# Selective-scan kernel on one core: another order of the sixteen states, three spread inflows, two decay tiles, six rows of C through a ring

## The chip, the cores and the metric

One core of a Trainium2 chip (trn2) runs the whole program. The metric is the device time of one execution in microseconds (us); lower is better.

## The reference, cut to what matters

A layer norm with modulation gives x_ssm (B=4 batches, 1024 tokens, 512 features). From it two selective state-space models are computed, one over the tokens forwards and one backwards, each with E=1024 channels and N=16 states a channel, and gated and projected back. The part that costs the time:

```
def _ssm(u, Wdbc, Wdt, bdt, Alog, Dp):
    dbc = einsum('bse,re->bsr', u, Wdbc);  dlt, Bm, Cm = split(dbc, [R, R + N])
    delta = softplus(einsum('bsr,er->bse', dlt, Wdt) + bdt)
    dA  = exp(delta[..., None] * -exp(Alog))                  # decay, N a channel
    dBu = delta[..., None] * Bm[:, :, None, :] * u[..., None] # inflow, N a channel
    h[t] = dA[t] * h[t-1] + dBu[t]                            # scan over t
    y[t] = sum over n of h[t, n] * C[t, n]                    # product and sum
    return y + u * Dp
out = x + gate * ((silu(mx) * (z1 + flip(z2))) @ Wf.T + bf + x_ssm)
```

## The kernel before, in words

All data is fp32, and everything around the scan is folded into it. A setup part (lines 28 to 485) folds weights, normalises tokens and writes the rows of B and C of each direction to DRAM. The main part (`ssm_kernel`) goes through 64 **units**. A unit k is one batch, one direction and 128 of the 1024 channels, with the 1024 tokens along the free axis: of each 16 units of a batch, the first 8 are forward in time and the next 8 backward. A unit has 16 **steps** c = 0 to 15, one for each state; q = 16k + c counts them through. Each engine has its own program, written out by hand as a loop over k and c with `if c == ...` for all side work; the engines meet only through semaphores, and each executes its own list strictly in order.

For a state four things are made: a decay (ScalarE, an exp of delta, line 1195), an inflow, a scan (VectorE, line 1326), and a product with the row of C, after which TensorE transposes it and adds it into the PSUM tile `y` (`sum_chunk`, line 885, four steps later, LAG). The string `KINDS` (line 487) says for each step how that is shared out:

- **E** (spread): TensorE makes the inflow by multiplying the transposed du with a diagonal matrix of B (`spread_inflow`, line 903; 8 products in fp32, which the trace shows as 16 instructions) into a PSUM slot. ScalarE makes the diagonals once a direction and batch (`make_diagonal`, line 1144, 8 instructions each).
- **A** (scaled): ScalarE scales the transposed du by B in two halves of four instructions (`scale_half`, line 1127, at the steps that `SCALE_STEPS` gives), and TensorE transposes the result into the slot (`turn_inflow`, line 893, 8 instructions).
- **V** and **P**: GpSimd multiplies the row of B, loaded by DMA into the ring `bst`, with du (line 1234). The decay goes into the PSUM slot.

For E and A the decay goes into the one tile `dec`, and GpSimd makes the product in place in `hbuf` (line 1239), as it does for P. For V VectorE scans into the slot and makes the product itself (line 1335). There are two slots; step q uses slot q % 2, so whatever writes it waits until step q - 2 has left it (`wait_scanned_out`, line 619): for a V that is the end of VectorE's product, for the others the end of the scan. `hbuf` is a ring of five. The 16 rows of C are resident in `cres` for a direction and batch, and are reloaded at its end (`load_c`, line 694, in SyncE's list); rows of B are loaded in a ring of four (`load_b`, line 688).

Side work in the same lists: the next unit's delta (TensorE at step 3; ScalarE's `softplus_start` and `softplus_end` at steps 4 and 5, right behind ScalarE's copy of the last y at step 4; VectorE's line 1260 at step 5, between the scan and the product of that step), and its z product (`z_part`), which feeds du (VectorE line 1270 and TensorE's `turn_du`, line 925). There are two kinds of unit:

- in **forward units** (k % 16 = 1 to 8) z is at steps 7 to 10, and an x product (`mx_part`, line 864) at steps 13, 14, 15 and the next 0. ScalarE makes its sigmoid in two halves, behind the decays of step 15 and of the next step 1 (`sigmoid_half`, line 1106), VectorE a silu from it.
- in **backward units** (k % 16 = 9 to 15 and 0) z is at steps 9 to 12; TensorE turns y back at step 7 for VectorE's gating at step 7 (line 1292), and makes the output projection of a token block (line 969) at steps 15 and the next 0, for which gated tiles are loaded in SyncE's list at step 13 (line 712), and of which VectorE reads the result at the next step 1. In the first batch work on B and C (`make_dbc`) stands in its place.

TensorE's list at a step is: the inflow of this state (A or E), skip terms at step 4, the sum of the state four steps back, then the side work.

Of the kernel before, what the change touches and what calls it, by code (L numbers as in the profile page):

```python
# [12 lines left out]
P = 128  # L13
# [3 lines left out]
ET = E // P  # L17
# [7 lines left out]
NU = 2 * B * ET  # L25


def setup_kernel(nc, t, scratch):

    with ExitStack() as ctx:  # L30
# [358 lines left out]
        def _(pe):  # L389
# [93 lines left out]
            for c in range(2):  # L483
# [3 lines left out]
KINDS = "EVAVEVAPAVAPAPAV"  # L487
SCALE_STEPS = {0: ((2, 0), (2, 1)), 3: ((6, 0),), 5: ((6, 1),), 6: ((8, 0),), 7: ((8, 1),), 8: ((10, 0),),
               9: ((10, 1),), 10: ((12, 0),), 11: ((12, 1),), 12: ((14, 0),), 13: ((14, 1),)}
SPREAD = [n for n in range(N) if KINDS[n] == "E"]  # L490
SEQ = ET * N
HR = 5
LAG = 4
DR = 2
# [25 lines left out]

INFLOWS_AT = {q: [i for i in range(DR, len(POOLED)) if inflow_step(i) == q] for q in range(NU * N)}


def ssm_kernel(nc, t, scratch):

    with ExitStack() as ctx:
# [3 lines left out]
        def sem(name):  # L530
# [3 lines left out]
        cres = sb("cres", [P, N, S])  # L534
# [3 lines left out]
        soft, ud, yrd, silu, ybuf, dec, dut = (sb(n, [P, S]) for n in (  # L538
            "soft", "ud", "yrd", "silu", "ybuf", "dec", "dut"))
# [14 lines left out]
        c_in = [sem(f"c_in{n}") for n in range(N)]  # L554
        last_in = sem("last_in")
# [60 lines left out]
        def z_bank(k, h):  # L616
            return mb[h] if k > 0 else y[:, half(h)]

# [52 lines left out]
        def _(sp):  # L671
# [22 lines left out]
            def load_c(g, n):  # L694
                sp.dma_start(cres[:, n, :],
                             scratch["bc"][g % 2, g // 2, N + n, :].partition_broadcast(P)).then_inc(c_in[n], 16)

# [39 lines left out]
            for n in range(3):  # L737
                load_c(0, n)

            for k in range(NU):  # L740
# [3 lines left out]
                for c in range(N):  # L744
# [4 lines left out]
                    if k == 0 and c + 3 < N:  # L749
                        load_c(0, c + 3)  # L750
                    if k == ET and c == 0:
                        sp.dma_start(wproj.rearrange("p a k r -> p (a k r)"), scratch["wproj"]).then_inc(pj_in, 16)
                        sp.dma_start(dbias, scratch["dbias"]).then_inc(pj_in, 16)
# [35 lines left out]
                    if k == NU - 1 and c >= ET:  # L789
                        wait_product(sp, q - ET)  # L790
                        sp.dma_start(skip_tile(TAIL + c - ET), scratch["xs"][NC - 2 + (c - ET) // TB, :, c % TB, :]).then_inc(rest_in, 16)
                        sp.dma_start(x_tile(TAIL + c - ET), t["xT"][TAIL + c - ET]).then_inc(rest_in, 16)
# [27 lines left out]
                    if e == ET - 1 and k + 1 < NU and c >= 5:  # L820
                        wait_product(sp, q - 5)
                        load_c(k // ET + 1, c - 5)
                    if e == 0 and k >= ET and c < 5:
                        wait_product(sp, q - 5)
                        load_c(k // ET, N - 5 + c)
# [255 lines left out]
        def _(act):  # L1081
# [94 lines left out]
            make_diagonal(0, 1)  # L1176

            for k in range(NU):
                f, zs = wtile(k), z_step(k)
                new_b = (k + 1) % ET == 0  # L1180
                for c in range(N):
# [3 lines left out]
                    if kind(q) in "AE":  # L1185
                        if before("AE", q) > 0:
                            act.wait_ge(scanned, TURNED[before("AE", q) - 1] + 1)
                        decays = dec[:]
# [10 lines left out]
                    if c == 1 and k > 0 and k % ET == 0:  # L1199
                        make_diagonal(k // ET, 1)  # L1200
# [27 lines left out]
        def _(pool):  # L1228
# [7 lines left out]
            def product(q):  # L1236
                pool.wait_ge(c_in[q % N], 16 * (q // SEQ + 1))
                pool.wait_ge(scanned, q + 1)
                nc.gpsimd.tensor_tensor(hbuf[:, q % HR, :], hbuf[:, q % HR, :], cres[:, q % N, :],  # L1239
                                        ALU.mult).then_inc(pool_prod, 1)  # L1240
# [14 lines left out]
        def _(dve):  # L1255
# [55 lines left out]
            for k in range(NU):  # L1311
                zs = z_step(k)
                step = -1 if backward(k) else 1
                for c in range(N):
                    q = N * k + c
                    dve.wait_ge(decay_ready, q + 1)
                    if kind(q) in "AE":
                        dve.wait_ge(turned, before("AE", q + 1))
                        decays, inflows = dec, slot[q % 2]
# [12 lines left out]
                    if kind(q) == "V":  # L1332
                        dve.wait_ge(scanned, q + 1)
                        dve.wait_ge(c_in[c], 16 * (q // SEQ + 1))
                        nc.vector.tensor_tensor(hbuf[:, q % HR, :], slot[q % 2][:], cres[:, c, :],  # L1335
# [91 lines left out]
```

## Time and profile before

| | |
|---|---|
| median of 3 runs | 3288.13 us (3287.22 to 3289.47) |
| profiled execution | 3287.01 us, its span 3285.2 us |
| busy: VectorE | 3017.2 us, 92% |
| busy: TensorE, matmuls | 2993.0 us, 91% |
| busy: GpSimd | 2903.7 us, 88% |
| busy: ScalarE | 2678.5 us, 82% |
| granted TensorE clock, mean | 0.985 of 2.4 GHz |
| moved by DMA | 560.40 MB |

The setup takes the first 255 us or so, up to the first scan, and what follows the last scan some 58 us. Between them lie the 64 units (unit 20, a forward one, and unit 28, a backward one, are looked at below; unit 8 is the first after a change of direction), so that 1 us more or less in every unit is 64 us. The profiled execution can be set against the median directly: they are 1.1 us apart.

### The profile page before, as it was taken

The page shows a single profiled execution, that of the slowest core. Times are in us where ns is not written, and L with a number is a line of the kernel's source. Part 1 is how long each engine was busy: PE and PEld are TensorE (multiplying, and loading weights), DVE is VectorE, ACT ScalarE, POOL GpSimd, SP SyncE. Part 2 cuts the span into 40 slices and gives each one's busy share as a digit, 9 for nine tenths or more (in the row PEclk, how much of TensorE's full clock was granted, in tenths as well). Part 3 has the DMA queues.
Part 4 walks back from the last instruction along what each step waited for, and adds up shares of the span by engine and source line. Part 5 has one row for each costly group of instructions (what it writes and reads, how often), then busy time and mean ns, then how long its engine had stood idle before and what let it go on. Part 6 is the DMA issues. An engine that isn't in the chain of part 4 may idle for free.

```text
span 3285.2 us, 54883 instructions
## 1 busy us (share of the span) xinstructions
PE 2993.0 (91%) x19924; PEld 2375.2 (72%) x19924; DVE 3017.2 (92%) x2008; ACT 2678.5 (82%) x5151; POOL 2903.7 (88%) x1288
## 2 busy tenths in 40 slices
PE   8887999899998999899999999899998999899999
PEld 5765666677677666678877767678777666677789
DVE  2838999999999999999999999999998999999994
ACT  1448999988888999987788999987877999988772
POOL 1528999999999999999999999999998999999993
PEclk9989999999999999999999999999999999999999
DMA  5775334644476333645465334645566343645463
GB/s 224 236 244 171 136 117 137 227 154 163 162 248 207 130 123 131 228 144 163 159 243 192 130 123 134 224 139 165 165 217 207 120 132 130 232 136 163 156 198 111
DMA packets 207053, 560.40 MB, mean 171 GB/s; under 512 B 20200, under 2 KB 66472, under 8 KB 202560
## 3 DMA queue, kind: packets, MB, share of 16 engines
q1 hardware_dynamic: 203424, 538.01, 48.5%
q0 software_dynamic: 2304, 16.78, 1.3%
q8 instruction: 159, 2.61, 0.3%
q10 hardware_dynamic: 1056, 2.10, 0.2%
q14 instruction: 110, 0.90, 0.1%
HBM read 476.19 MB, written 80.63 MB: 169 GB/s over the span
## 4 chain that ended last, share of the span: by engine, by line
PE 49%; ACT 20%; DVE 12%; issue 10%; POOL 1%; DVEq 0%; ACTq 0%; POOLq 0%
PE y L888 14%; PE slot L899 10%; PE mb L859 9%; ACT abuf L1134 8%; PE mb L969 6%; DVE hbuf L1326 6%; ACT slot L1195 3%; DVE hbuf L1335 3%; PE mb L869 3%; PE slot L911 3%; DVE slot L1326 3%; ACT dec L1195 2%; PE mb L930 1%; ACT soft L1090 1%; ACT yrd L1125 1%
## 5 line engine op out<-in xcount | busy, mean ns | idle before, releaser
L1239 POOL TENSOR_TENSOR hbuf<-hbuf,cres 128x1024 f32<-128x1024 f32 x704 | 1664.4, 2377 | 143.9 <-DVE hbuf L1326 143.8
L1234 POOL TENSOR_TENSOR bst<-bst,du 128x1024 f32<-128x1024 f32 x512 | 1220.2, 2383 | 46.7 <-DVE du L1270 46.7
L1326 DVE TENSOR_TENSOR_SCAN hbuf<-dec,slot 128x1024 f32<-128x1024 f32 x512 | 1165.0, 2275 | 40.3 <-PE slot L911 27.2
L888 PE MATMUL y<-ident,hbuf 128*128 128x128 f32 x8192 | 1016.0, 273 | 1.8 <-POOL hbuf L1239 1.7
L888 PEld LDWEIGHTS y<-ident,hbuf 128*128 128x128 f32 x8192 | 923.9, 141 | 106.4 <-issue 103.5
L1134 ACT ACTIVATE abuf<-dut,bt 128x128 f32<-128x128 f32 x3072 | 964.7, 387 | 0.0
L1326 DVE TENSOR_TENSOR_SCAN slot<-slot,bst 128x1024 f32<-128x1024 f32 x320 | 728.3, 2276 | 22.5 <-ACT slot L1195 22.1
L1195 ACT ACTIVATE slot<-delta,par 128x1024 f32<-128x1024 f32 x512 | 568.4, 1110 | 199.6 <-DVE hbuf L1335 186.6
L1195 ACT ACTIVATE dec<-delta,par 128x1024 f32<-128x1024 f32 x512 | 584.2, 1141 | 118.7 <-DVE hbuf L1326 118.1
L899 PE MATMUL slot<-ident,abuf 128*128 128x128 f32 x3072 | 408.6, 276 | 170.8 <-ACT abuf L1134 160.1
L899 PEld LDWEIGHTS slot<-ident,abuf 128*128 128x128 f32 x3072 | 339.0, 141 | 303.4 <-ACT abuf L1134 243.0
L859 PE MATMUL mb<-xn,wzs 128*128 128x512 f32 x1008 | 478.9, 597 | 15.2 <-DVE ybuf L1292 11.7
L1326 DVE TENSOR_TENSOR_SCAN hbuf<-slot,bst 128x1024 f32<-128x1024 f32 x192 | 434.7, 2264 | 0.1
L1335 DVE TENSOR_TENSOR hbuf<-slot,cres 128x1024 f32<-128x1024 f32 x320 | 390.7, 1221 | 8.0
L911 PEld LDWEIGHTS slot<-diag,dut 128*128 128x128 f32 x2048 | 260.2, 203 | 106.3 <-issue 102.9
L911 PE MATMUL slot<-diag,dut 128*128 128x128 f32 x2048 | 269.6, 288 | 43.0 <-DVE hbuf L1326 40.1
L859 PEld LDWEIGHTS mb<-xn,wzs 128*128 128x128 f32 x1008 | 171.6, 190 | 146.3 <-issue 144.2
L869 PE MATMUL mb<-xn,wx 128*128 128x512 f32 x512 | 240.9, 593 | 0.0
L969 PE MATMUL mb<-ybuf,wf 128*128 128x128 f32 x1504 | 179.0, 278 | 5.0 <-issue 4.1
L969 PEld LDWEIGHTS mb<-ybuf,wf 128*128 128x128 f32 x1504 | 174.6, 194 | 5.4 <-issue 4.3
L848 PE MATMUL mb<-dl,wdt 81*128 81x512 f32 x256 | 135.1, 632 | 17.2 <-DVE silu L1280 10.0
L869 PEld LDWEIGHTS mb<-xn,wx 128*128 128x128 f32 x512 | 87.3, 190 | 61.2 <-issue 61.2
(157 smaller groups left out, 2301.3 us busy)
## 6 DMA issues: line engine op xcount, KB each, us to landing
bst<-bc_s SPq DMA_DIRECT2D x512, 512.0 KB, 3.9
cres<-bc_s SPq DMA_DIRECT2D x128, 512.0 KB, 6.8
wzs<-wz_s SPq DMA_DIRECT2D x64, 256.0 KB, 4.0
yf_s<-yrd SPq DMA_DIRECT2D x32, 512.0 KB, 5.3
ybuf<-yf_s SPq DMA_DIRECT2D x32, 512.0 KB, 4.8
yg_s<-ybuf SPq DMA_DIRECT2D x31, 512.0 KB, 4.4
si_s<-silu SPq DMA_DIRECT2D x28, 512.0 KB, 6.1
silu<-si_s SPq DMA_DIRECT2D x28, 512.0 KB, 5.4
```

Of the source, the lines that this page charges most:

```text
L859: last = nc.tensor.matmul(z_bank(k, h), wz[:, i * P:(i + 1) * P], xn[:, h, i, :], start=(i == 0), stop=(i == DT - 1))
L869: last = nc.tensor.matmul(mb[h], wx[:, i * P:(i + 1) * P], xn[:, h, i, :], start=(i == 0), stop=(i == DT - 1))
L888: last = nc.tensor.matmul(y[:, j * P:(j + 1) * P], hbuf[:, q % HR, j * P:(j + 1) * P], ident[:], start=False, stop=(q % N == N - 1), is_tr ...
L899: last = nc.tensor.matmul(slot[q % 2][:, j * P:(j + 1) * P], abuf[:, a % 2, j * P:(j + 1) * P], ident[:], start=True, stop=True, is_transp ...
L911: last = nc.tensor.matmul(slot[q % 2][:, j * P:(j + 1) * P], dut[:, j * P:(j + 1) * P], diag[:, i, j, :], start=True, stop=True)
L969: nc.tensor.matmul(bank[:, m * P:(m + 1) * P], wf[:, e, m * P:(m + 1) * P], tokens, start=(e == 0 and m == 0), stop=False, skip_group_chec ...
L1134: last = nc.scalar.activation(abuf[:, a % 2, j * P:(j + 1) * P], dut[:, j * P:(j + 1) * P], ACT.Copy, scale=bt[:, g % 2, j, n:n + 1])
L1195: nc.scalar.activation(decays, delta[:, k % 2, :], ACT.Exp, scale=par[:, f // ET, f % ET, PA + c:PA + c + 1]).then_inc(decay_ready, 1)
L1234: nc.gpsimd.tensor_tensor(bst[:, i % BR, :], bst[:, i % BR, :], du[:, k % 2, :], ALU.mult).then_inc(pool_b, 1)
L1239: nc.gpsimd.tensor_tensor(hbuf[:, q % HR, :], hbuf[:, q % HR, :], cres[:, q % N, :], ALU.mult).then_inc(pool_prod, 1)
L1326: nc.vector.tensor_tensor_scan(h[:, ::step], decays[:, ::step], inflows[:, ::step], 0.0, ALU.mult, ALU.add).then_inc(scanned, 1)
L1335: nc.vector.tensor_tensor(hbuf[:, q % HR, :], slot[q % 2][:], cres[:, c, :], ALU.mult).then_inc(dve_prod, 1)
```

## The change

`KINDS` becomes `EVAPEVAAEVAPAVAP`, from `EVAVEVAPAVAPAPAV`. A unit then has three spread states (steps 0, 4, 8), six scaled (2, 6, 7, 10, 12, 14), four V (1, 5, 9, 13) and three P (3, 11, 15), where it had two, six, five and three. `SCALE_STEPS` is rewritten for them. A third tile of diagonals is made by ScalarE, before the first unit and at step 3 of every eighth. `dec` becomes a ring of two, so that a decay waits for the scan of two such states back. Of the 16 rows of C ten stay resident (`KEPT`) and six (`STREAMED`: steps 0, 3, 5, 8, 11, 13) go in every unit through a ring of three tiles; SyncE loads the next one five steps after the step whose product frees the tile. The lists of TensorE, VectorE and GpSimd are otherwise untouched; they read `KINDS`.

The diff, cut to its core:

```diff
-KINDS = "EVAVEVAPAVAPAPAV"
-SCALE_STEPS = {0: ((2, 0), (2, 1)), 3: ((6, 0),), 5: ((6, 1),), 6: ((8, 0),), 7: ((8, 1),), 8: ((10, 0),),
-               9: ((10, 1),), 10: ((12, 0),), 11: ((12, 1),), 12: ((14, 0),), 13: ((14, 1),)}
+KINDS = "EVAPEVAAEVAPAVAP"
+SCALE_STEPS = {0: ((2, 0), (2, 1)), 2: ((6, 0),), 3: ((6, 1),), 5: ((7, 0),), 6: ((7, 1),), 7: ((10, 0),),
+               8: ((10, 1),), 9: ((12, 0),), 10: ((12, 1),), 11: ((14, 0),), 12: ((14, 1),)}
 SPREAD = [n for n in range(N) if KINDS[n] == "E"]
...
+STREAMED = (0, 3, 5, 8, 11, 13)
+KEPT = [n for n in range(N) if n not in STREAMED]
+CR = 3
+DECS = 2
...
+STREAM = [q for q in range(NU * N) if q % N in STREAMED]
...
-        cres = sb("cres", [P, N, S])
+        cres = sb("cres", [P, len(KEPT) + CR, S])
...
+        dec = sb("dec", [P, DECS, S])
...
+        def stream_index(q):
+            return q // N * len(STREAMED) + STREAMED.index(q % N)
+
+        def c_tile(q):
+
+            if q % N in STREAMED:
+                return cres[:, len(KEPT) + stream_index(q) % CR, :]
+            return cres[:, KEPT.index(q % N), :]
+
+        def wait_c(eng, q):
+            if q % N in STREAMED:
+                eng.wait_ge(cs_in[stream_index(q) % CR], 16 * (stream_index(q) // CR + 1))
+            else:
+                eng.wait_ge(c_in[q % N], 16 * (q // SEQ + 1))
...
+            def load_streamed(i):
+                q = STREAM[i]
+                g = q // SEQ
+                sp.dma_start(cres[:, len(KEPT) + i % CR, :],
+                             scratch["bc"][g % 2, g // 2, N + q % N, :].partition_broadcast(P)).then_inc(cs_in[i % CR], 16)
...
+                    if q >= 5 and (q - 5) % N in STREAMED and stream_index(q - 5) + CR < len(STREAM):
+                        wait_product(sp, q - 5)
+                        load_streamed(stream_index(q - 5) + CR)
...
-                        wait_product(sp, q - ET)
+                        wait_product(sp, N * k + KEPT[c - ET])
...
-                    if e == ET - 1 and k + 1 < NU and c >= 5:
+                    if e == ET - 1 and k + 1 < NU and c - 5 in KEPT:
                         wait_product(sp, q - 5)
                         load_c(k // ET + 1, c - 5)
-                    if e == 0 and k >= ET and c < 5:
+                    if e == 0 and k >= ET and c < 5 and N - 5 + c in KEPT:
...
             make_diagonal(0, 1)
+            make_diagonal(0, 2)
...
                     if kind(q) in "AE":
-                        if before("AE", q) > 0:
-                            act.wait_ge(scanned, TURNED[before("AE", q) - 1] + 1)
-                        decays = dec[:]
+                        if before("AE", q) >= DECS:
+                            act.wait_ge(scanned, TURNED[before("AE", q) - DECS] + 1)
+                        decays = dec[:, before("AE", q) % DECS, :]
...
-                    if c == 1 and k > 0 and k % ET == 0:
-                        make_diagonal(k // ET, 1)
+                    if c in (1, 3) and k > 0 and k % ET == 0:
+                        make_diagonal(k // ET, (c + 1) // 2)
...
-                        decays, inflows = dec, slot[q % 2]
+                        decays, inflows = dec[:, before("AE", q) % DECS, :], slot[q % 2]
```

## Rows read from the trace of the kernel before

**Rows 1.** Busy time in stretches: unit 8 from 630.4, unit 28, unit 20.

```profile
core 0: us, PE busy (x) PEld busy (x) DVE busy (x) ACT busy (x) POOL busy (x), PEclk, DMA share, GB/s
630.40:637.20 6.80, 5.26 (x25) 5.19 (x25) 6.22 (x4) 6.62 (x11) 4.70 (x2) 0.50 0.69 215
...
1543.90:1590.60 46.70, 43.38 (x331) 37.35 (x329) 45.69 (x29) 37.49 (x73) 44.31 (x20) 1.00 0.48 160
1174.70:1220.20 45.50, 41.45 (x262) 30.77 (x261) 44.97 (x26) 42.47 (x82) 44.26 (x20) 1.00 0.36 129
```

**Rows 2.** Timeline of VectorE, unit 20 (start us, us, engine, line, op, tiles, count).

```profile
1174.73 2.30 DVE L1326 TENSOR_TENSOR_SCAN slot<-slot,bst 128x1024 f32<-128x1024 f32 x1 [0.38 <-ACT slot L1195]
...
1186.70 2.27 DVE L1326 TENSOR_TENSOR_SCAN slot<-slot,bst 128x1024 f32<-128x1024 f32 x1
...
1190.01 1.21 DVE L1335 TENSOR_TENSOR hbuf<-slot,cres 128x1024 f32<-128x1024 f32 x1
1191.13 2.27 DVE L1326 TENSOR_TENSOR_SCAN hbuf<-dec,slot 128x1024 f32<-128x1024 f32 x1
1193.33 2.26 DVE L1326 TENSOR_TENSOR_SCAN hbuf<-slot,bst 128x1024 f32<-128x1024 f32 x1
...
1220.23 2.30 DVE L1326 TENSOR_TENSOR_SCAN slot<-slot,bst 128x1024 f32<-128x1024 f32 x1 [0.37 <-ACT slot L1195]
```

**Rows 3.** Timeline of TensorE, unit 20.

```profile
1193.62 1.09 PE L899 MATMUL slot<-ident,abuf 128*128 128x128 f32 x8 [1.43 <-ACT abuf L1134]
1194.55 1.04 PE L888 MATMUL y<-ident,hbuf 128*128 128x128 f32 x8
1195.42 1.88 PE L859 MATMUL mb<-xn,wzs 128*128 128x512 f32 x4
...
1212.94 1.04 PE L888 MATMUL y<-ident,hbuf 128*128 128x128 f32 x8
...
1215.53 1.95 PE L911 MATMUL slot<-diag,dut 128*128 128x128 f32 x16
```

**Rows 4.** Timeline of ScalarE, unit 20.

```profile
1173.60 1.10 ACT L1195 ACTIVATE slot<-delta,par 128x1024 f32<-128x1024 f32 x1
...
1181.18 1.15 ACT L1195 ACTIVATE dec<-delta,par 128x1024 f32<-128x1024 f32 x1 [0.54 <-DVE hbuf L1326]
...
1185.15 1.10 ACT L1195 ACTIVATE slot<-delta,par 128x1024 f32<-128x1024 f32 x1
...
1213.14 0.69 ACT L1109 ACTIVATE soft<-mb,par 128x512 f32<-128x512 f32 x1 [0.72 <-PE mb L869]
...
1216.76 2.43 ACT L1134 ACTIVATE abuf<-dut,bt 128x128 f32<-128x128 f32 x8
1219.10 1.10 ACT L1195 ACTIVATE slot<-delta,par 128x1024 f32<-128x1024 f32 x1
```

**Rows 5.** Timeline of VectorE, unit 28: scans of steps 0, 8, next 0.

```profile
1543.89 2.29 DVE L1326 TENSOR_TENSOR_SCAN hbuf<-dec,slot 128x1024 f32<-128x1024 f32 x1 [0.56 <-PE slot L911]
...
1568.65 2.27 DVE L1326 TENSOR_TENSOR_SCAN hbuf<-dec,slot 128x1024 f32<-128x1024 f32 x1
...
1590.61 2.29 DVE L1326 TENSOR_TENSOR_SCAN hbuf<-dec,slot 128x1024 f32<-128x1024 f32 x1 [0.56 <-PE slot L911]
```

**Rows 6.** Timeline of TensorE, unit 28.

```profile
1571.07 1.07 PE L899 MATMUL slot<-ident,abuf 128*128 128x128 f32 x8 [0.24 <-DVE hbuf L1326]
...
1584.55 0.60 PE L930 MATMUL mb<-ident,du 128*128 128x128 f32 x4
```

**Rows 7.** Timeline of ScalarE, unit 28.

```profile
1551.01 1.12 ACT L1195 ACTIVATE slot<-delta,par 128x1024 f32<-128x1024 f32 x1 [3.65 <-DVE hbuf L1335]
...
1557.18 1.10 ACT L1195 ACTIVATE slot<-delta,par 128x1024 f32<-128x1024 f32 x1
```

**Rows 8.** Timeline of TensorE, unit 8.

```profile
629.37 1.12 PE L848 MATMUL mb<-dl,wdt 81*128 81x512 f32 x2 [2.49 <-DVE silu L1280]
...
632.04 3.75 PE L911 MATMUL slot<-diag,dut 128*128 128x128 f32 x16 [1.54 <-DVE hbuf L1326]
```

More of the change, by code:

```diff
@@ L537, in ssm_kernel @@
         delta, du = (sb(n, [P, 2, S]) for n in ("delta", "du"))
-        soft, ud, yrd, silu, ybuf, dec, dut = (sb(n, [P, S]) for n in (
-            "soft", "ud", "yrd", "silu", "ybuf", "dec", "dut"))
+        soft, ud, yrd, silu, ybuf, dut = (sb(n, [P, S]) for n in (
+            "soft", "ud", "yrd", "silu", "ybuf", "dut"))
+        dec = sb("dec", [P, DECS, S])
         abuf = sb("abuf", [P, 2, S])
@@ L554, in ssm_kernel @@
         c_in = [sem(f"c_in{n}") for n in range(N)]
+        cs_in = [sem(f"cs_in{i}") for i in range(CR)]
         last_in = sem("last_in")
@@ L694, in load_c @@
             def load_c(g, n):
-                sp.dma_start(cres[:, n, :],
+                sp.dma_start(cres[:, KEPT.index(n), :],
                              scratch["bc"][g % 2, g // 2, N + n, :].partition_broadcast(P)).then_inc(c_in[n], 16)
+            def load_streamed(i):
[3 more added lines that the diff above has]
+                             scratch["bc"][g % 2, g // 2, N + q % N, :].partition_broadcast(P)).then_inc(cs_in[i % CR], 16)
             def load_forward_y(k):
@@ L735, in store_dbc @@
                                  dbc[R:RD, d, :]).then_inc(dbc_out, 16)
-            for n in range(3):
+            load_streamed(0)
+            for n in (1, 2):
                 load_c(0, n)
+            for i in range(1, CR):
+                load_streamed(i)
             for k in range(NU):
@@ L748, in _ @@
                         load_b(before("VP", q - 2) + BR)
-                    if k == 0 and c + 3 < N:
+                    if k == 0 and c + 3 in KEPT:
                         load_c(0, c + 3)
+                    if q >= 5 and (q - 5) % N in STREAMED and stream_index(q - 5) + CR < len(STREAM):
+                        wait_product(sp, q - 5)
+                        load_streamed(stream_index(q - 5) + CR)
                     if k == ET and c == 0:
@@ L1236, in product @@
             def product(q):
-                pool.wait_ge(c_in[q % N], 16 * (q // SEQ + 1))
+                wait_c(pool, q)
                 pool.wait_ge(scanned, q + 1)
-                nc.gpsimd.tensor_tensor(hbuf[:, q % HR, :], hbuf[:, q % HR, :], cres[:, q % N, :],
+                nc.gpsimd.tensor_tensor(hbuf[:, q % HR, :], hbuf[:, q % HR, :], c_tile(q),
                                         ALU.mult).then_inc(pool_prod, 1)
@@ L1333, in _ @@
                         dve.wait_ge(scanned, q + 1)
-                        dve.wait_ge(c_in[c], 16 * (q // SEQ + 1))
-                        nc.vector.tensor_tensor(hbuf[:, q % HR, :], slot[q % 2][:], cres[:, c, :],
+                        wait_c(dve, q)
+                        nc.vector.tensor_tensor(hbuf[:, q % HR, :], slot[q % 2][:], c_tile(q),
                                                 ALU.mult).then_inc(dve_prod, 1)
```

## The prediction

> **What bounds the kernel now.** I read first the stretches of one unit of each type, for the engines' shares, then the timelines of VectorE, TensorE and ScalarE inside them. Times below are offsets in us; S(c) is the start of the scan of step c. In a forward unit VectorE is busy 44.97 of 45.5 us, GpSimd 44.26, ScalarE 42.47, TensorE 41.45; in a backward unit 45.69, 44.31, 37.49 and 43.38 of 46.7 [rows 1]. Read alone, that says that VectorE is the bound and that each product taken from it is won. The timelines say something narrower.
>
> Forward unit. S(1) is at 1174.73 and again at 1220.23, 45.50 a pass [rows 2], and the pass goes round a ring. TensorE finishes the first half of the x product at 1212.94 [rows 3]; ScalarE, which has waited 0.72 for it, makes the sigmoid, the decay of step 0, two halves of a scaling and the decay of step 1, and only then can scan 1 start, at 1220.23, after a wait of 0.38: 7.29 in all [rows 4]. From S(1) to S(6) VectorE sets the pace, 16.40 [rows 2]. 2.49 later TensorE starts the transposes of state 8 [rows 3] and works almost without a gap until the x product: 19.32. The sum, 7.29 + 16.40 + 2.49 + 19.32 = 45.50, is the unit. So three engines are in series, each with almost no slack, although VectorE's idle is only 0.5.
>
> Backward unit. S(0) to S(8) is 24.76, S(8) to the next S(0) 21.96 [rows 5]. TensorE starts state 10 when scan 8 is done (wait 0.24), and from the transposes of the second half of du, at 1584.55, goes on through half a projection and the spreading of state 0 to S(0), 6.06 later, for which VectorE waits 0.56 [rows 5, 6].
>
> **The change, part by part.**
>
> *One product fewer on VectorE.* 1.21 of work [rows 2], some 1.27 of VectorE's time with the gap behind the scan (estimate from the same rows): 64 x 1.27 = 81 us if VectorE alone counted. On GpSimd a product comes and an inflow goes (12 + 7 for 11 + 8 operations), so that nothing changes, with over 1 us of idle a unit to spare [rows 1].
>
> *Step 7 becomes a scaled state.* Until now all of these stood at even steps, whose slot only scans of E and A states read. Step 7's slot holds the scan of step 5, a V state: its transposes wait for the product of step 5, which VectorE makes behind delta and ends 0.09 after S(6) [rows 2]. With 0.15 of signal time (estimate: TensorE's start 1571.07 lies 0.15 behind the end of scan 8 at 1570.92 [rows 5, 6]) TensorE starts at S(6) + 0.24. Queued behind it: 0.93 transposes, 0.87 sum of state 3, 1.71 of the next unit's z product (each printed length less the 0.17 by which it overlaps what follows), then 1.78 for spreading state 8 [rows 3], and some 0.27 to its scan (estimate: the 0.17 of tail and a signal). So S(8) = S(6) + 5.80, where two scans want 4.40 [rows 2]: 1.40 of stall in every forward unit. In backward units a gating of 1.1 lies between the scans and most of it is hidden: 0.35.
>
> *TensorE's part of the forward ring* grows accordingly. It was 2.49 + 19.32 from S(6). Now it is 0.24 + 5.29 + (19.32 - 0.93) = 23.92: +2.11. The third spread state (16 instructions where a scaled one has 8) is in this.
>
> *Scaling of state 6 a step earlier, two decay tiles.* ScalarE goes from the decay of step 1 (1173.60) to that of step 5 (1185.15) in 11.55, 0.54 of it a wait that the second decay tile removes [rows 4]. One more half scaling comes in, 1.17 (two took 2.34 [rows 4]): 12.18. VectorE would need 11.97 - 1.27 = 10.70 for S(1) to S(5) [rows 2]. So ScalarE takes over, and S(1) to S(6) is 12.18 + 4.43 = 16.61 instead of 16.40: the whole product saved at step 3 is lost, +0.21. The tiles buy nothing more, since decays of V and P states still go into slots.
>
> *V at 13, not 15.* Forward: the decay of step 15 now waits for the product of step 13, and is ready about when the x product is (S(13) + 4.6 against + 4.7, estimates by the same lengths): 0, next late if TensorE gets faster. Forward ring: 7.29 + 16.61 + 23.92 = 47.82, **+2.3**.
>
> Backward: the product at step 15 stood behind du's second half and hid TensorE's 6.06; at 13 it stands ahead of du. TensorE's path stays, VectorE's cover shrinks by 1.27, the wait before S(0) grows from 0.56 to 1.83: S(8) to S(0) is 21.96 + 1.27 = 23.23. In the first half step 3 saves 1.27; but ScalarE needs 1558.28 - 1551.01 = 7.27 from the decay of step 3 to that of step 5 [rows 7], where VectorE would now want 6.45: -1.27 + 0.85 + 0.35 (step 8) makes 24.7. Sum 47.9, **+1.2**.
>
> *Third diagonal.* Eight more scalings of the form of [rows 4], 2.34, at step 3, just ahead of the decay of step 5: at the start (2.3, nothing hides it), in units 16, 32, 48 in full, in units 8, 24, 40, 56 about 4.0 with the forward loss (0.6 hidden).
>
> *C through the ring.* 336 more loads of C, 64 fewer of B: +143 MB. The DMA share is 0.36 to 0.48 in these units [rows 1]; 13 loads for 8 is some 0.6 to 0.7. A tile is asked for at step q+5 and used 3 to 4 steps later, over 8 us; I take 0. With the cover gone it is the load of gated tiles, now behind a C load in SyncE's queue at step 13 of 23 units, about 1 us each. SyncE's new waits are for products five steps old; behind them stand loads of B whose own waits end later. 0.
>
> First sum: 28 forward units x 2.3 = 65, 4 x 4.0 = 16, 31 backward x 1.2 = 37, 3 x 2.3 = 7, start and unit 0 4 = 129: 3287 + 129 = **3416**.
>
> **The clock.** TensorE finishes state 2's sum about 3.2 before the product of step 5 lets it go on (forward: the skip terms wait for ScalarE's copy of y, S(1) + 9.0, and five groups of eight of 0.87 follow, so S(1) + 13.4; the start is at S(1) + 12.18 + 4.43 + 0.24 = S(1) + 16.85, which leaves 3.2 to 3.4; backward, by the same steps, 16.1 and 19.1 from S(0)), where now two waits near 1.4 stand, with z work between [rows 3]. In unit 8 TensorE waited 2.49 and 1.54, and the granted clock was 0.50, 1.2 GHz, from 630.4 to 637.2; 16 spreading instructions took 3.75 instead of 1.95 [rows 1, 3, 8]. What follows the new wait is TensorE's critical stretch. Bounds a unit: 0, and 2.6 (3.75 - 1.95, and again 0.8 for the next eight). The nearest row is the wait of 2.49, so the clock should fall; but low time may begin inside the wait, and in some units not at all. I take 1.2: x 62 = 74. **3416 + 74 = 3490.** The Trainium skill, page "TensorE: Matmul & The Clock Gate", section "HAM oscillation — how this bites in real kernels", describes a loop that waits once a turn and is re-throttled in every turn; by that rule the price is 2.6 in all units, and the sum 3577. No row here shows a wait of this length recurring each unit.
>
> The profiled execution took 3287.0, the median of the runs 3288.1; the 1.1 between them is within what I claim. 0.2% is about what a measurement of this kernel can tell from no change.
>
> **Rivals.**
> - *The clock holds.* Waits of 1.2 to 1.5 in a unit go by at 2.4 GHz [rows 1, 3]. Then 3416. Chance 0.26.
> - *The clock falls everywhere and for long*, or tiles of C or gated y are late besides: 62 x 2.6: 3577. Chance 0.12.
> - *Faster: the rings open.* If scaling and decays run far enough ahead that scan 1, scan 5 and the backward S(0) never wait (it decides at the 0.38 and 0.56 waits: they must vanish, not grow), what is left is VectorE's work plus the step-8 stall: forward 45.50 - 1.27 - 0.38 + 1.40, -0.25 x 32; backward 46.72 - 1.27 - 0.91 + 0.35, -1.8 x 31: 3223. For it speaks VectorE's 99% [rows 1]; against it that the series of [rows 2 to 4] closes to 0.01 us. Chance 0.07.
> - *Gains and stalls cancel*: 3288. Chance 0.03.
>
> **How the numbers follow.** Main case 0.52: 3490. Range: down to the held clock less 26 (3390), up to 3580; that leaves out 0.10 below and part of the 0.12 above. Faster 0.07, same 0.03, slower 0.90.
>
> **What would show it.** Forward units of about 49 us and at least 47.8; scan 8 waiting for TensorE L911 in forward units; scan 5 waiting for ScalarE L1195; backward S(0) waiting 1.8; TensorE waiting about 3 us before L899 for the product L1335, and 0.50 in the granted clock behind it; VectorE at about 87%. Wrong if forward units stay below 46, or scan 8 starts without a wait; the clock's part is wrong if the low stretches are as few as now.

## The result, and the profile after

The changed kernel takes 3474.85 us, median of 4 runs (3462.63 to 3476.64); the kernel before took 3287.68 on the same chip. The ratio is 1.0563, 95% interval [1.055, 1.0576]: slower by 5.6%. Forecast were 3490, between 3390 and 3580. The profiled execution took 3476.64, its span 3474.8.

The page of the changed kernel:

```profile
span 3474.8 us, 57210 instructions
...
PE 3150.8 (91%) x20948; PEld 2567.4 (74%) x20948; DVE 2960.5 (85%) x1944; ACT 2690.1 (77%) x5215; POOL 2909.3 (84%) x1288
...
q1 hardware_dynamic: 242592, 680.64, 58.9%
```

VectorE has 57 us less to do than before (3017.2) and the program is 190 longer. TensorE's busy time rose by 158, which is not only the third spread state: part of it is the same work at the lower clock, as the rows of unit 21 below show. The groups by line, with what ended the idle time before them, say who waits now:

```profile
L1363 DVE TENSOR_TENSOR_SCAN hbuf<-dec,slot 128x1024 f32<-128x1024 f32 x576 | 1309.0, 2279 | 224.5 <-PE slot L947 102.6 <-issue 48.7 <-ACT slot L1232 41.8
...
L1363 DVE TENSOR_TENSOR_SCAN slot<-slot,bst 128x1024 f32<-128x1024 f32 x256 | 584.3, 2282 | 64.3 <-ACT slot L1232 49.4 <-PE y L924 14.9
...
L935 PE MATMUL slot<-ident,abuf 128*128 128x128 f32 x3072 | 425.9, 284 | 185.2 <-DVE hbuf L1372 175.5 <-ACT abuf L1170 8.3 <-DVE hbuf L1363 1.5
```

The first two are VectorE's scans (L1326 before), the third TensorE's transposes of scaled inflows (L899 before). The scans waited 63 us in all before (40.3 and 22.5), and wait 289 now: for the spreading of inflows (L947), for ScalarE's decays (L1232). The transposes wait 175.5 for VectorE's product (L1372, before L1335). Each of the three engines waits for another: a ring, as before, only longer.

Where the 190 lie, from the starts of the scans of step 0: the first scan comes 1.6 later (257.0 for 255.4); unit 0 is 3.9 longer; the 28 forward units take 1369 instead of 1283 (+86); the four last forward ones, units 8, 24, 40 and 56, take 213 instead of 193 (+20); 30 backward ones 1480.4 instead of 1402.8 (+78; units 0 and 63 are not among them). After the last scan nothing changed (60.0).

A forward unit (20) at full clock. VectorE, to be read beside [rows 2]:

```profile
1239.09 2.29 DVE L1363 TENSOR_TENSOR_SCAN hbuf<-dec,slot 128x1024 f32<-128x1024 f32 x1 [0.51 <-issue]
1241.75 2.30 DVE L1363 TENSOR_TENSOR_SCAN slot<-slot,bst 128x1024 f32<-128x1024 f32 x1 [0.38 <-ACT slot L1232]
...
1250.42 2.29 DVE L1363 TENSOR_TENSOR_SCAN hbuf<-dec,slot 128x1024 f32<-128x1024 f32 x1
1253.72 2.30 DVE L1363 TENSOR_TENSOR_SCAN slot<-slot,bst 128x1024 f32<-128x1024 f32 x1 [1.01 <-ACT slot L1232]
1255.92 1.21 DVE L1297 SCALAR_TENSOR_TENSOR delta<-mb,soft 128x1024 f32<-128x1024 f32 x1
1257.05 1.21 DVE L1372 TENSOR_TENSOR hbuf<-slot,cres 128x1024 f32<-128x1024 f32 x1
1258.17 4.45 DVE L1363 TENSOR_TENSOR_SCAN hbuf<-dec,slot 128x1024 f32<-128x1024 f32 x2
...
1263.94 2.29 DVE L1363 TENSOR_TENSOR_SCAN hbuf<-dec,slot 128x1024 f32<-128x1024 f32 x1 [1.31 <-PE slot L947]
...
1289.18 2.30 DVE L1363 TENSOR_TENSOR_SCAN slot<-slot,bst 128x1024 f32<-128x1024 f32 x1 [0.37 <-ACT slot L1232]
```

New waits: 1.01 before scan 5, 1.31 before scan 8, and 0.51 before scan 0. The last moves nothing, because the old wait of 0.38 before scan 1, for ScalarE, still stands behind it. The row of 4.45 is scans 6 and 7. TensorE in the same unit, beside [rows 3]:

```profile
1254.34 1.04 PE L924 MATMUL y<-ident,hbuf 128*128 128x128 f32 x8
1258.40 1.06 PE L935 MATMUL slot<-ident,abuf 128*128 128x128 f32 x8 [3.02 <-DVE hbuf L1372]
1259.30 1.04 PE L924 MATMUL y<-ident,hbuf 128*128 128x128 f32 x8
1260.18 1.88 PE L895 MATMUL mb<-xn,wzs 128*128 128x512 f32 x4
1261.90 1.95 PE L947 MATMUL slot<-diag,dut 128*128 128x128 f32 x16
```

The transposes of state 7 wait 3.02 for the product that ends at 1258.26, and the sum of state 3, the z product and the spreading of state 8 queue behind them. One unit later the same rows read:

```profile
1305.83 1.94 PE L935 MATMUL slot<-ident,abuf 128*128 128x128 f32 x8 [3.02 <-DVE hbuf L1372]
1307.56 1.92 PE L924 MATMUL y<-ident,hbuf 128*128 128x128 f32 x8
1309.26 3.09 PE L895 MATMUL mb<-xn,wzs 128*128 128x512 f32 x4
1312.19 1.95 PE L947 MATMUL slot<-diag,dut 128*128 128x128 f32 x16
```

The wait is the same, 3.02, but now each operation takes nearly twice as long. The busy times in stretches, with the granted clock behind the busy times (columns as in [rows 1]), say why:

```profile
1254.30:1261.90 7.60, 4.58 (x31) 3.42 (x30) 7.60 (x5) 7.37 (x16) 7.17 (x4) 1.00 0.98 342
...
1304.90:1311.70 6.80, 5.87 (x19) 4.48 (x20) 5.24 (x3) 6.57 (x15) 6.41 (x4) 0.50 0.93 274
1239.10:1286.50 47.40, 42.64 (x279) 32.71 (x277) 44.02 (x25) 42.27 (x81) 44.28 (x20) 1.00 0.52 178
1286.50:1336.80 50.30, 45.55 (x279) 34.84 (x278) 44.13 (x25) 42.35 (x81) 44.34 (x20) 0.93 0.54 169
```

Unit 20 ran at 2.4 GHz throughout and took 47.4; unit 21 had 1.2 GHz (0.50) from 1304.9, inside the wait, to 1311.7 and took 50.3. The forward units come in three levels, 47.4, 49.0 and 50.3, by how long the lower clock lasted in them. From the first scan to the last, 235 us lie at the lower clock, in 44 of the 64 units; before it was 65 us in 12 units. Of the 50 stretches at the lower clock, 36 begin within 1.4 us of the end of TensorE's wait for the product of step 5, which is 3.02 long, or 2.86 in most backward units that project. In the kernel before, unit 8 and its like are not the only ones: in six forward units (4, 7, 35, 37, 51, 54) a stretch at 1.2 GHz begins within 0.6 of the end of a wait of 1.16, while the same wait passes at 2.4 GHz 23 times.

A backward unit (28), beside [rows 5], the scans of steps 0, 5 and next 0:

```profile
1638.87 2.29 DVE L1363 TENSOR_TENSOR_SCAN hbuf<-dec,slot 128x1024 f32<-128x1024 f32 x1 [5.52 <-issue]
...
1653.29 2.30 DVE L1363 TENSOR_TENSOR_SCAN slot<-slot,bst 128x1024 f32<-128x1024 f32 x1 [0.25 <-PE y L924]
...
1663.54 2.29 DVE L1363 TENSOR_TENSOR_SCAN hbuf<-dec,slot 128x1024 f32<-128x1024 f32 x1 [0.22 <-ACT slot L1232]
...
1686.75 2.29 DVE L1363 TENSOR_TENSOR_SCAN hbuf<-dec,slot 128x1024 f32<-128x1024 f32 x1 [1.79 <-ACT slot L1232]
```

and TensorE at the end of the unit and, in the first row, of the unit before it:

```profile
1631.55 5.44 PE L1005 MATMUL mb<-ybuf,wf 128*128 128x128 f32 x32 [1.86 <-issue]
...
1680.64 0.66 PE L966 MATMUL mb<-ident,du 128*128 128x128 f32 x4 [0.28 <-DVE du L1307]
1681.14 3.74 PE L1005 MATMUL mb<-ybuf,wf 128*128 128x128 f32 x32
1684.71 1.95 PE L947 MATMUL slot<-diag,dut 128*128 128x128 f32 x16
```

(1663.54 is scan 8.) The wait ahead of the next unit's scan 0 was 0.56 and is 1.79. The profile names ScalarE's decay, which is long done; what came last is TensorE's spreading of state 0, from 1684.71 for 1.95. TensorE itself waited 0.28 for the second half of du, which VectorE makes behind its product of step 13: here VectorE sets the end of the unit.

The 5.52 before the first row is another matter. In unit 27 the projection waited 1.86 for its gated tiles, which landed 8.2 after their issue (the median is 6.5), and from 1632.5 to 1636.0 the granted clock was 0.50, so that it took 5.44 instead of 3.74. Unit 27 took 51.6 instead of 47.9.

### The profile page after: what moved, and what is told of

It reads as the page before. It is cut to its first block and busy times, and to the rows that moved or that the text cites. A ratio compares the mean times of both kernels' runs of the same rounds, so it can differ in the third digit from the quotient of the medians.

```text
span 3474.8 us, 57210 instructions
## 1 busy us (share of the span) xinstructions
PE 3150.8 (91%) x20948; PEld 2567.4 (74%) x20948; DVE 2960.5 (85%) x1944; ACT 2690.1 (77%) x5215; POOL 2909.3 (84%) x1288
## 5 line engine op out<-in xcount | busy, mean ns | idle before, releaser
L1276 POOL TENSOR_TENSOR hbuf<-hbuf,cres 128x1024 f32<-128x1024 f32 x768 | 1811.3, 2375 | 329.1 <-DVE hbuf L1363 328.1
L1363 DVE TENSOR_TENSOR_SCAN hbuf<-dec,slot 128x1024 f32<-128x1024 f32 x576 | 1309.0, 2279 | 224.5 <-PE slot L947 102.6
L1271 POOL TENSOR_TENSOR bst<-bst,du 128x1024 f32<-128x1024 f32 x448 | 1069.6, 2388 | 47.0 <-DVE du L1307 47.0
L1232 ACT ACTIVATE slot<-delta,par 128x1024 f32<-128x1024 f32 x448 | 496.3, 1108 | 349.1 <-DVE hbuf L1372 349.1
L1232 ACT ACTIVATE dec<-delta,par 128x1024 f32<-128x1024 f32 x576 | 655.5, 1138 | 23.2 <-DVE hbuf L1363 23.2
L1363 DVE TENSOR_TENSOR_SCAN slot<-slot,bst 128x1024 f32<-128x1024 f32 x256 | 584.3, 2282 | 64.3 <-ACT slot L1232 49.4
L935 PE MATMUL slot<-ident,abuf 128*128 128x128 f32 x3072 | 425.9, 284 | 185.2 <-DVE hbuf L1372 175.5
L947 PEld LDWEIGHTS slot<-diag,dut 128*128 128x128 f32 x3072 | 379.4, 198 | 126.8 <-issue 123.5
L947 PE MATMUL slot<-diag,dut 128*128 128x128 f32 x3072 | 391.3, 282 | 47.8 <-DVE hbuf L1363 45.0
L1372 DVE TENSOR_TENSOR hbuf<-slot,cres 128x1024 f32<-128x1024 f32 x256 | 312.3, 1220 | 5.8
L1139 ACT ACTIVATE ud<-mb,par 128x512 f32<-128x512 f32 x126 | 97.4, 773 | 135.7 <-PE mb L895 135.7
L1005 PE MATMUL mb<-ybuf,wf 128*128 128x128 f32 x1504 | 178.5, 277 | 4.3 <-issue 2.2
L1005 PEld LDWEIGHTS mb<-ybuf,wf 128*128 128x128 f32 x1504 | 173.5, 193 | 5.7 <-ACT dut L1195 2.8
```

The costliest lines, as they stand in the source:

```text
L935: last = nc.tensor.matmul(slot[q % 2][:, j * P:(j + 1) * P], abuf[:, a % 2, j * P:(j + 1) * P], ident[:], start=True, stop=True, is_transp ...
L947: last = nc.tensor.matmul(slot[q % 2][:, j * P:(j + 1) * P], dut[:, j * P:(j + 1) * P], diag[:, i, j, :], start=True, stop=True)
L1005: nc.tensor.matmul(bank[:, m * P:(m + 1) * P], wf[:, e, m * P:(m + 1) * P], tokens, start=(e == 0 and m == 0), stop=False, skip_group_chec ...
L1232: nc.scalar.activation(decays, delta[:, k % 2, :], ACT.Exp, scale=par[:, f // ET, f % ET, PA + c:PA + c + 1]).then_inc(decay_ready, 1)
L1271: nc.gpsimd.tensor_tensor(bst[:, i % BR, :], bst[:, i % BR, :], du[:, k % 2, :], ALU.mult).then_inc(pool_b, 1)
L1363: nc.vector.tensor_tensor_scan(h[:, ::step], decays[:, ::step], inflows[:, ::step], 0.0, ALU.mult, ALU.add).then_inc(scanned, 1)
```

## The experiments

Twelve kernels ran. All times are medians; the ratio is to the kernel before on the same chip. Offsets are from a unit's own scan 0, S(c) is the start of scan c.

**1. The new buffers without the new order.** The kernel after, with the old `KINDS` and `SCALE_STEPS` and two diagonals; the ring of C and the two decay tiles stay.

```diff
-KINDS = "EVAPEVAAEVAPAVAP"
+KINDS = "EVAVEVAPAVAPAPAV"
```

> The changed kernel with the old order of kinds, the old scaling steps and two diagonals, but with the ring for six rows of C and the two decay tiles. Theory A (the loss is in the order of the states: TensorE, ScalarE and VectorE in series): 3288 us, at most 8 either way, forward units at 45.5, backward at 46.7, the granted clock back at 0.985; the 143 MB more and the second decay tile are worth nothing. Rival B (the additional loads of C delay something in every unit): over 3400 us, with waits that end on a DMA.

Measured: 3322.44, ratio 1.0109 [1.0092, 1.0126]. The order carries 152 of the 187 us, but the buffers are not free under the old order. Forward units are as before (45.5), and so are the backward ones of the first batch (45.6); those with a projection are 48.0 instead of 46.7. SyncE's queue, then TensorE, in unit 28 of this kernel:

```profile
1582.76 0.32 SPq L715 DMA_DIRECT2D bst<-bc_s  x1
1583.13 0.43 SPq L725 DMA_DIRECT2D cres<-bc_s  x1
1583.60 0.43 SPq L743 DMA_DIRECT2D ybuf<-yg_s  x1
```

```profile
1590.05 3.81 PE L1005 MATMUL mb<-ybuf,wf 128*128 128x128 f32 x32 [0.91 <-ACT dut L1195]
```

The gated tiles are asked for behind a row of B and a row of C, and the projection starts 6.45 after the issue, having waited 0.91. (The profile names ScalarE's dut, which was there at 1589.78; the load landed at 1589.96.) Theory A's 3288 was missed by 34 us. Rival B had the kind of cause right, a load that comes late, and its price, over 100 us, wrong.

**2. The gated load one step earlier**, the rest as in 1.

```diff
-                    if c == 13 and block_now is not None and k < NU - 1:
+                    if c == 12 and block_now is not None and k < NU - 1:
```

> x1_old_order (old order of kinds, C ring, two decay tiles), with SyncE's load of gated tiles moved from step 13, behind the loads of B and C, to step 12. x1 measured 3322 us, with backward units of the last three batches at 48.0 instead of 46.7, the projection starting 6.4 us after its load was issued. Theory A2 (that load, late behind a C load, is all that the C ring costs): 46.7 again in these units, 3290, between 3284 and 3298. Rival (the 143 MB slow something else): no better than 3315.

Measured: 3281.31, ratio 0.9987 [0.9978, 0.9996]. The load is issued at 1577.88, the projection starts at 1587.53 without a wait, and these units are 46.7 again. Unit 47, which took 54.5 before the change too, takes 48.4. So the whole loss of experiment 1 was the place of one load in SyncE's queue. Two things come together in it: the issue is some 0.5 later (0.84 behind the row of B for 0.36), and the load takes a median of 6.5 from issue to landing where it took 5.5 in the kernel before. The 143 MB are not what slows it: experiment 10, without the ring of C, has 6.6, behind a row of B and two other loads.

**3. V at 15 again**, the rest of the change kept.

```diff
-KINDS = "EVAPEVAAEVAPAVAP"
+KINDS = "EVAPEVAAEVAPAPAV"
```

> The changed kernel with its fourth V state at step 15 and a P at 13, where they stood before the change. Theory A: the product at 15 covers TensorE's projection and spreading again, so the wait before the backward scan 0 falls from about 1.8 to 0.56 us and a backward unit from 47.9 to 46.6; forward units stay at 47.4; 30 x 1.27 = 38 us less, about 3437. Rival C (the backward unit is simply as long as TensorE's work with the third spread state): no change, 3475.

Measured: 3466.1, ratio 1.0543 [1.0523, 1.0563]: only 9 of the 38 us expected. Forward units stay as they were (1368 us in all). In unit 28 the step from S(8) to the next S(0) is 22.93, not 21.96. Either the late load of experiment 1 or something else holds it; experiment 6 separates them.

**4. The wait of 3 us broken.** Eight transposes of the identity at step 6, after delta is there, into a PSUM tile that is free then. They compute nothing that is used.

```diff
+                    if c == 6 and 0 < k < NU - 1:
+                        pe.wait_ge(delta_ready, k + 2)
+                        for j in range(ET):
+                            nc.tensor.matmul(mb[0][:, 0:P], ident[:], ident[:], start=True, stop=True, is_transpose=True)
```

> Eight transposes of the identity more in each unit, into a bank that is free, on TensorE between the sum of step 6 and the transposes of step 7, behind delta, so that the wait of 3 us there is broken; nothing else changes, and the added work ends before the product that TensorE waits for. Theory A with the clock: forward units stay at their 47.4 and backward ones at 47.9 in (nearly) all units, where now 2 in 3 are longer by 1.6 to 2.9; 60 to 85 us less, 3390 to 3415, granted clock about 0.98. Rival D (the long units have another cause, the wait is not what lowers the clock): 3475 or more.

Measured: 3410.94, ratio 1.0381 [1.0365, 1.0396]: more work, 64 us less. TensorE at that place, now waiting 1.80 and then a moment:

```profile
1235.14 1.09 PE L1082 MATMUL mb<-ident 128*128 128x128 f32 x8 [1.80 <-DVE delta L1301]
1236.36 1.06 PE L935 MATMUL slot<-ident,abuf 128*128 128x128 f32 x8
```

The time at the lower clock falls from 235 to 71 us (15 units instead of 44), and the median forward unit is 47.43. TensorE still starts state 7 at S(6) + 0.23, so its part of the ring is untouched: the gain is the clock, 64/164 = 0.39 us of time for each us no longer at 1.2 GHz. By that price the clock's share of the change, 170 us more at 1.2 GHz than before, is 66 (an estimate).

**5. The queued work moved ahead of the wait.** The first quarter of z, in forward units, and the turning of y, in backward ones, stand at step 6.

```diff
-                    if c == 7 and gates(k):
+                    if c == 6 and gates(k):
...
+                        if c == 6 and zs == 7:
+                            z_part(k + 1, 0, range(0, 2))
+                        if (zs + 1 if zs == 7 else zs) <= c < zs + 4:
```

> TensorE makes the first quarter of z (forward units) and turns y back (backward units) at step 6, in the wait, instead of behind the transposes of step 7. Theory A: TensorE starts step 7 at S(6)+0.9 instead of +0.24 but has 1.7 less to do behind it: forward ring 47.4 - 1.05 = 46.4, the wait of scan 8 falls from 1.3 to about 0.3; backward -0.3; and the clock holds in most units. 3475 - 85 - 30 - 10 = 3350, between 3335 and 3375. Rival E (scan 8 waits for the third spread state itself, whatever stands before it): wait of scan 8 unchanged at 1.3.

Measured: 3375.76, ratio 1.0274 [1.0257, 1.0291], 99 us off and the best version that keeps the new order. S(6) to S(8) is 4.68 instead of 5.76, forward units at full clock take 46.35, backward ones that project 47.6, and 105 us are at the lower clock. The 3350 expected was too low by 26: it put the clock at 85, and the 130 us fewer at 1.2 GHz are worth 51 at the price of experiment 4.

**6. Fill, V at 15 and the early load together.**

> The changed kernel with the fill of x3 in TensorE's wait, the fourth V at step 15 instead of 13, and the load of gated tiles at step 12. x2 (V at 15 alone) gained 9 us instead of 38: theory A2 says that two things stood in the way, the late load of gated tiles in the units that project, and the low clock in the others. With both out of the way backward units are at 46.6 instead of the 47.9 of x3, forward ones stay at 47.4: 3411 - 38 = 3373, between 3365 and 3385. Rival C (a backward unit is as long as TensorE's work): 3411.

Measured: 3400.65, ratio 1.0347 [1.033, 1.0365], outside the 3365 to 3385 expected. With the load early, the backward unit falls only from 47.9 to 47.4, 0.5 of the 1.27. TensorE's row in unit 28 of this kernel, and VectorE's scans of step 8 and next 0:

```profile
1635.11 1.04 PE L935 MATMUL slot<-ident,abuf 128*128 128x128 f32 x8
```

```profile
1631.90 2.29 DVE L1367 TENSOR_TENSOR_SCAN hbuf<-dec,slot 128x1024 f32<-128x1024 f32 x1 [0.22 <-ACT slot L1236]
...
1654.62 2.29 DVE L1367 TENSOR_TENSOR_SCAN hbuf<-dec,slot 128x1024 f32<-128x1024 f32 x1 [1.31 <-PE slot L947]
```

Before, TensorE started state 10 at S(8) + 2.42 and waited for it [rows 5, 6]. Here it starts at S(8) + 3.21, without a wait: it is late itself, by 0.79, since the transposes of state 7, the turning of y and 16 spreading instructions are now one row of work. From there to S(0) TensorE has no wait, and from S(8) to S(0) are 22.72 = 21.96 + 0.76. With V at 15 TensorE's lateness thus shows at the unit's end in full. In the changed kernel, with V at 13, the order is the reverse: TensorE waits for du there, and its own lateness is a second limit, 0.5 behind the first.

**7. ScalarE's extra scaling cut.** Experiment 4 with three of the four instructions of state 6's first half left out from unit 1 on, so that this part of the inflow is not computed.

```diff
-                for j in range(TB * h, TB * h + TB):
+                for j in range(TB * h, TB * h + (1 if (n, h) == (6, 0) and q >= N else TB)):
```

> x3_fill_wait with three of the four instructions of the first half scaling of state 6 left out from unit 1 on (ScalarE, step 2, 0.88 us less). Theory A (in forward units ScalarE sets the way from scan 1 to scan 5): the wait of scan 5 falls from 1.0 to about 0.1 and a forward unit from 47.4 to 46.6; a backward unit stays at 47.9, since there ScalarE waits for the product of step 1 behind this scaling: 3411 - 32 x 0.88 = 3383. Rival (only TensorE's and VectorE's parts count): 3411.

Measured: 3384.06, ratio 1.0302 [1.0287, 1.0317]; forward units at full clock take 46.55, 0.88 less than the 47.43 of experiment 4. The time taken from ScalarE comes out in full. It does so too in backward units of the first batch (46.8 for 47.7), which I had not expected, and not at all in those with a projection (47.9). ScalarE's decay of step 3, behind the cut scaling, in experiment 4's units 12 (first batch) and 28 says why:

```profile
840.73 1.10 ACT L1236 ACTIVATE slot<-delta,par 128x1024 f32<-128x1024 f32 x1
...
1615.85 1.12 ACT L1236 ACTIVATE slot<-delta,par 128x1024 f32<-128x1024 f32 x1 [5.32 <-DVE hbuf L1376]
```

In unit 12 ScalarE works from step 1 to step 5 without a wait, having begun late (3.98 for TensorE's work on B and C); in unit 28 it waits 5.32 for VectorE's product right behind that scaling, and a shorter scaling only makes this wait longer.

**8. VectorE relieved, nothing else.** The kernel before; from unit 1 on the product of step 3 covers 128 of 1024 columns, the rest of that product being left out.

```diff
+                        w = P if c == 3 and k > 0 else S
```

> The kernel before with VectorE's product at step 3 over 128 of the 1024 columns from unit 1 on, about 1.0 us of VectorE's work less a unit, and nothing else changed. Theory A (VectorE's time counts only until the next engine is late, ScalarE's decay of step 5): a forward unit gains 0.4 to 0.5, a backward one 0.5 to 0.6, about 32 us in all: 3255. Rival F (VectorE, busy 99% of a forward unit, is the bound): 1.0 a unit, 64 us, 3223.

Measured: 3267.67, ratio 0.9947 [0.9932, 0.9962], 17 us less where 32 were expected, and far from rival F's 64. With 0.94 less work (0.29 for 1.23), forward units fall by 0.40 (45.10) and backward ones by 0.39 (46.33). Most of the rest is a new wait two scans on, at scan 5 of unit 20:

```profile
1182.21 2.30 DVE L1326 TENSOR_TENSOR_SCAN slot<-slot,bst 128x1024 f32<-128x1024 f32 x1 [0.43 <-ACT slot L1195]
```

**9. The link of 2.49 in the forward ring.** The kernel before, both halves of state 8's scaling at step 6.

```diff
-5: ((6, 1),), 6: ((8, 0),), 7: ((8, 1),), 8: ((10, 0),),
+5: ((6, 1),), 6: ((8, 0), (8, 1)), 8: ((10, 0),),
```

> The kernel before with both half scalings of state 8 at step 6, instead of one at 6 and one at 7 (ScalarE had 0.64 us of idle between them, waiting for a product; TensorE then waited 1.4 for the second). Theory A (the forward unit is a ring through TensorE's start of state 8): TensorE can start up to 1.7 us earlier, the wait of 0.38 at scan 1 goes, forward units go from 45.5 to 45.1, backward ones stay at 46.7: 12 us less, 3273. Rival: nothing, since VectorE is at 99% already and TensorE is not the bound: 3285.

Measured: 3286.83, ratio 1.000 [0.9991, 1.0009]: the 12 us of theory A did not come, and forward units stay at 45.50. TensorE at state 8 of unit 20, where [rows 3] had 1.43 for ScalarE's `abuf`:

```profile
1193.18 1.06 PE L899 MATMUL slot<-ident,abuf 128*128 128x128 f32 x8 [1.37 <-DVE hbuf L1326]
```

The wait has changed its releaser and lost 0.06. Scan 6 reads the slot until 1193.02, so S(6) + 2.43 is as early as this place can be in this order of the states.

**10 and 11. The same edit with the early load**, in the kernel before (10) and under experiment 2's buffers (11).

> b1_scale_8_at_6 and the load of gated tiles at step 12 instead of 13. Theory A2: besides b1's 12 us the one long unit (54.5, at the change into the last batch, where TensorE waited 4 us for that load and went on at half clock) falls to about 48.4: 18 us less than before, 3267.

> y1_old_order_early_gated (C ring, two decay tiles, old order, early load) with both half scalings of state 8 at step 6. Theory A: 12 us less than y1's 3281, 3269, the same as b4, since the ring of C and the second decay tile are worth nothing in either direction.

Measured: 3281.32, ratio 0.9987 [0.9979, 0.9996], and 3281.74, ratio 0.9988 [0.998, 0.9997]. Expected were 3267 and 3269. The load alone gives this (experiment 9 without it: nothing; experiment 2 without the scaling: the same 3281); the scaling gives nothing in either. That the two agree says that with the load early the C ring and the second decay tile neither cost nor bring anything under the old order, although 143 MB more are moved.

**12. The other end of the ring.** The kernel before, the early load, and the second half scaling of state 2 behind the decay of step 1.

```diff
-SCALE_STEPS = {0: ((2, 0), (2, 1)), 3: ((6, 0),), ...
+SCALE_STEPS = {0: ((2, 0),), 1: ((2, 1),), 3: ((6, 0),), ...
```

> The kernel before, with two edits: the load of gated tiles at step 12 instead of 13 (its worth is known from two earlier runs, 3281 us, since unit 47 no longer runs long), and the second half scaling of state 2 made behind ScalarE's decay of step 1 instead of ahead of it. Theory (the forward unit is a closed ring in which scan 1 is released by the decay of step 1, last): the decay comes 1.17 us earlier, the wait of 0.37 us ahead of scan 1 goes, since scan 0 ends then, and everything behind S(1) moves with it: forward units 45.5 -> 45.1, 28 of them some 10 us, time 3271 (3267 to 3275). Rival (as when the scaling of state 8 was moved, a second wait lies right behind this one, in scan 0, which TensorE's spreading of state 0 releases, or in TensorE's transposes of state 2, which now want the later half): the wait is gone, the unit stays 45.5, time 3281.

Measured: 3263.71, ratio 0.9927 [0.9914, 0.9941], the fastest of all, 7 us below the 3271 expected. VectorE at the place of the 0.37 of [rows 2]:

```profile
1214.62 2.29 DVE L1326 TENSOR_TENSOR_SCAN hbuf<-dec,slot 128x1024 f32<-128x1024 f32 x1
1216.82 2.27 DVE L1326 TENSOR_TENSOR_SCAN slot<-slot,bst 128x1024 f32<-128x1024 f32 x1
```

and the whole forward unit in the view of busy times:

```profile
1169.60:1214.60 45.00, 41.17 (x263) 30.83 (x262) 44.86 (x26) 42.34 (x81) 44.24 (x20) 1.00 0.39 132
```

The wait is gone, the unit is 45.0, and VectorE is busy 44.86 of it: only here does VectorE set the pace almost alone. The 28 forward units together take 1269 us (1283 before), and units 8, 24, 40 and 56 take 190 (193); that and the load are the gain. The time at the lower clock is down to 31 us.

## Why the prediction was right, point by point

**The direction and the size** came out: 3475 for 3490. Taken part by part, the errors are small, some of them cancel, and some reasons were incomplete.

**Forward ring at full clock**: 47.43 for 47.8. Its three parts: S(1) to S(6) 16.42 for 16.61; S(6) to the sum that follows the first half of the x product (1281.88) 23.71 for 23.92; from there to S(1) 7.30 for 7.29. Step 7's stall was 1.31 for 1.40, TensorE's start at S(6) + 0.23 for 0.24. That V at 13 would be free here was right: ScalarE's sigmoid follows the decay of step 15 without a wait, at S(13) + 4.62, when TensorE's x product has just ended, and experiment 3, with V at 15, left forward units as they were.

**The product taken from VectorE is lost in waits**: shown twice. In the changed kernel scan 5 waits 1.01 for ScalarE and S(1) to S(6) is no shorter than before; in experiment 8 VectorE's relief alone gives 0.4 of 0.94. With it falls the rival "the rings open", and the reading of VectorE's 99% as the bound. Experiment 7 shows the other side: time taken from ScalarE counts one for one. The prediction said that the ring has almost no slack; for VectorE it was 0.4 us, and the new scaling used it up.

**Backward unit**: 47.89 for 47.9; S(0) to S(8) 24.67 for 24.7, S(8) to S(0) 23.22 for 23.23, the wait 1.79 for 1.83. The mechanism "VectorE's cover shrinks by 1.27" was true, as TensorE's wait for du shows, and not the whole: in experiment 6 the cover is back and only 0.5 returns, since TensorE comes 0.79 late out of step 8. I had worked out that its list behind the 3-us wait is longer, for the forward unit, and had carried it in the backward one no further than scan 8 (0.35). And +1.2 holds only for the units that project: the seven of the first batch go from 45.63 to 47.66 at full clock, +2.03. ScalarE, which starts late there behind the work on B and C, sets the way from S(1) to S(6) and makes it longer (16.59 for 16.12), where in unit 28 it is shorter (16.68 for 17.07).

**Units 8, 24, 40, 56**: +4.95 each, clock included, for 4.0 and the clock's 1.2. Start and unit 0: 1.6 + 3.9 = 5.5 for 4.

**The clock**: 66 for 74, by experiment 4's price. The place was right: the wait was forecast at 3.2 and is 3.02, and the granted clock is 0.50 from inside it on. The mean forward unit lies 1.46 above the held 47.43; before, it lay 0.31 above 45.50 (45.81), so +1.15 for 1.2. Backward ones lie 1.51 above their mean at full clock (49.35 for 47.84, both kinds together), before 0.29 (46.76 for 46.47, nearly all of it unit 47 with 54.5). That these means come so near 1.2 is in part luck: the 1.2 was chosen between the bounds 0 and 2.6, and it covers units with nothing beside units with more than the upper bound. A unit like 21 loses 2.9. The remark that waits of 1.2 to 1.5 go by at 2.4 GHz holds in most units and not in all, as the six units with a wait of 1.16 show.

The rival "the clock holds" (3416) is out by the result and by experiment 4, which comes down to 3411 with the clock mostly held. The Trainium skill, page "TensorE: Matmul & The Clock Gate", section "HAM oscillation — how this bites in real kernels", has a loop that waits some 3 to 5 us for a DMA at every turn and is re-throttled at every turn. The trace agrees only in part: a wait of about 3 us recurs in unit after unit (3.02 in units 20 and 21), and 20 of the 64 units have no low stretch.

So the sum at held clock was 3416 where 3475 - 66 = 3409 was right (an estimate, as the 66 is). The forward units give 28 x 0.37 = 10 less than forecast, the first batch's backward ones 7 x 0.8 = 6 more, the start 1.5 more; some 4 less lie in terms that no run separates. These 7 and the 8 of the clock are the error of 15.

**C through the ring at 0.** In the changed kernel that holds nearly: TensorE's projection (L1005) waited 4.3 us in the whole run, 1.86 of it in unit 27, which then ran 3.4 us at 1.2 GHz and lost 3.7. The remark that the gated load would be next, "about 1 us each in 23 units", once the cover is gone, had the price right (1.2 to 1.3 each) and the condition wrong: it struck with the old order, cover in place (31.6 us of waits of L1005 in experiment 1), where the path of TensorE was short enough to reach the load; in the changed kernel V at 13 and TensorE's own lateness push the projection behind the load. An early load alone was not tried there.

**The signs named.** Forward units are at 49.04 in the median, but those at full clock at 47.43, under the 47.8 named as the least. VectorE is at 85% for the 87% forecast. The waits came where they were forecast.

**Still open**: why the same wait of 3.02 leaves the clock at 2.4 GHz in unit 20 and not in unit 21.

## What to carry to other kernels

An engine at 99% is the bound only if the others' waits say so too: close the ring first, link by link, in the timelines, and test each link by the second wait that stands right behind the first (experiment 9 failed on one, experiment 12 found one with nothing behind it: a half scaling moved by one step gave 0.5%). When an instruction is placed where its input comes late, count all that queues behind it on its engine, up to the end of the unit. A load that lands just in time has no room for one more load ahead of it in its queue: here that made it 0.5 later and 1 us slower (experiment 1). Issuing it one step earlier cost nothing and made the memory ring free.

## What the runs showed of the hardware that was not expected

Eight transposes of 0.87 us in all, in the middle of a wait of 3 us, kept TensorE at 2.4 GHz in most units: 235 us at the lower clock became 71, and useless work made the kernel 64 us faster. The wait of 3.02 is identical in units 20 and 21, and one of them pays 2.9 us for it. And the gated tiles, issued 0.84 us behind a row of B and 0.47 behind a row of C, land a median of 6.5 after their issue (experiment 1), where they took 5.5 in the kernel before, behind a row of B alone.
